# First attention of a six-layer decoder kernel: slot scores made in turned layout, two heads in the two 64-column halves of the array

## The chip, the cores and the metric

One core of a Trainium2 chip. The metric is the device time of one execution of the whole kernel in microseconds (us), as the median over runs.

## The reference, cut to what matters

The kernel computes a decoder with two layers on an input of 4 x 256 tokens of width 256: a gated slot attention, a state-space scan over a context, a mixture of experts, a linear attention, a cross attention and a quantized feed-forward block, each followed by a layer norm. The change is in the first of these, the slot attention with 16 heads, key width 64, value width 128 and 64 slots:

```python
z = cumlogsumexp(s, axis=time)          # s: slot logits, clipped
p, g = exp(s - z), exp(z_prev - z)
hk = hk * g + k_t p_t                   # first recurrence, read by q
ok_t = q_t * scale @ hk                 # one row of 64 slots per head
pv = softmax(ok, axis=slots)
hv = hv * g + p_t v_t                   # second recurrence
ov_t = pv_t @ hv
```

Written without the recurrence: with e = exp(s) and z = the running sum of e over time, ok of a query at time t is (sum over keys up to t of (q.k) e) divided by z, slot by slot. The softmax over slots follows, its weights are divided by z again, and ov is (sum over keys up to t of (w.e) v). So there are two divisions by the same z: one of ok before the maximum, one of the softmax weights before they are used.

## The kernel before, in words

The first attention runs over 8 pairs of heads, `step` once per pair (a loop of 7 and a last one), and each engine has its own `step` with its instructions in a fixed order; semaphores tie them. Woven into the same eight steps, on VectorE, ScalarE and GpSimd, is the scan of the second layer (`scan`, `decay_of`, `drive_of`, `read_of`), four scans of 128 x 1024 in each step. PSUM is used as four areas of two banks: PJ, AB, X and Y.

TensorE, in a step of pair i: it turns eT, the exponentials of the slot logits with the slots of two heads in the partitions, into tokens in the partitions (line 606, into X); ScalarE copies them to `e_tok`. Then it projects values and gates of the eight token tiles, `project_vg(t)` (line 617), into the two banks of PJ in turn, each of which must have been emptied by ScalarE (`v`, `th`) and by VectorE (`gate(t-2)`). After tiles 0 and 1 come eight turns of the logarithm of z (line 629, into Y), then the slot scores (lines 639 to 641, into X): for each sequence and head three products with 128 columns of masked scores `aT` as the stationary operand and 64 columns of `e_tok` streaming, an output with tokens in the partitions. Every float32 product is two instructions here, so these are 48. Then tiles 2 to 7 of `project_vg`, then, once VectorE's `w_ready` has come, eight turns of the weights `okn` (line 651, into Y), which ScalarE copies to `wT`. Then for each sequence `read` (line 582, the second use of scores, eT against wT), VectorE's mask (line 1563) and `mix` (lines 671 to 673), the next pair's `project_qks` (572), turns of the output (692), the output projection (703) and the next pair's scores (582).

ScalarE makes `z_inv` = exp(-ln z) from the turned logarithm (line 1265, 2 x 512 columns), the values and tanh of the gates for each tile, `slot_exp` (line 1271) between tiles 3 and 4, and `wT` (line 1279). The page shows nearly all ScalarE work under line 1216, its helper. The logarithm itself is taken in `log_sums`, at the end of the step before.

VectorE: `gate(0)`, `gate(1)`, the scan of line 1552, then okn = slot scores x z_inv (1588), the maximum over each 64 slots (1590), the subtraction of it (1593), the weights okn = slot_exp x z_inv (1598), the sum (1600) and a small product `eps_sq` (1604), with gates between, then the masks.

GpSimd does the products and sums of the layer-2 scan; in `steps` it waits for `w_ready`, the end of line 1598, before the first `read_of`.

Of the kernel before, what the change touches and what calls it, by code (L numbers as in the profile page):

```python
# [16 lines left out]
P = 128  # L17
# [50 lines left out]
def at(i, per, c):  # L68

    return i * per + c  # L70


def build(nc, a, out):

    with ExitStack() as ctx:
# [3 lines left out]
        def sb(name, shape, dt=F32):  # L79
            return mem[-1].enter_context(nc.sbuf_tensor(name, shape, dt))  # L80
# [33 lines left out]
        zT = sb("zT", [P, TOK])  # L114
        z_inv = sb("z_inv", [P, TILES, P])
        aT = sb("aT", [P, 8, 384])
# [185 lines left out]
        e_copied = sem("e_copied")  # L302
        z_turned = sem("z_turned")
        zi_ready = sem("zi_ready")
        slots_ready = sem("slots_ready")
        slots_shifted = sem("slots_shifted")
        slots_exp = sem("slots_exp")
        w_ready = sem("w_ready")
        tanh_ready = sem("tanh_ready")
# [246 lines left out]
        def _(pe):  # L556
# [40 lines left out]
            def step(i, last_pair):  # L597
# [25 lines left out]

                pe.wait_ge(lnz_ready, at(i, 1, 1))
                pe.wait_ge(scores_masked, at(i, 4, 4))
                for n in range(2):
                    for t in range(4):
                        c = (4 * n + t) * P
                        last = nc.tensor.transpose(ps[:, Y + n, t * P:(t + 1) * P], zT[:, c:c + P], ident[:])
                    last.then_inc(z_turned, 1)  # L630

                pe.wait_ge(e_copied, at(i, 2, 2))
                for b in range(B):
                    for h in range(2):
                        n = 2 * b + h
                        m = slice(M * h, M * h + M)
                        o0 = ps[:, X + b // 2, (b % 2) * 256 + M * h:(b % 2) * 256 + M * h + M]
                        o1 = ps[:, X + b // 2, (b % 2) * 256 + P + M * h:(b % 2) * 256 + P + M * h + M]
                        mm(o0, aT[:, n, 0:P], e_tok[:, 2 * b, m], start=True, stop=True)
                        mm(o1, aT[:, n, P:256], e_tok[:, 2 * b, m], start=True, stop=False)  # L640
                        last = mm(o1, aT[:, n, 256:384], e_tok[:, 2 * b + 1, m], start=False, stop=True)
                last.then_inc(slots_ready, 1)
                for t in range(2, TILES):
                    project_vg(t)

                pe.wait_ge(w_ready, at(i, 1, 1))
                pe.wait_ge(zi_ready, at(i, 2, 2))
                for n in range(2):
                    for t in range(4):
                        r = 4 * n + t  # L650
                        last = nc.tensor.transpose(ps[:, Y + n, t * P:(t + 1) * P],
                                                   okn[:, 2 * r:2 * r + 2, :].rearrange("p a b -> p (a b)"), ident[:])
                    last.then_inc(w_turned, 1)
# [456 lines left out]
        def _(pool):  # L1110
# [14 lines left out]
            def steps(i, last_pair):  # L1125
                def read_of(n):

                    j, e = n // 2, n % 2
                    pool.wait_ge(scanned, at(i, 4, n + 3))
                    G.tensor_tensor(state[:, n % 2], state[:, n % 2], c_row[:, j], ALU.mult).then_inc(read_out, 1)  # L1130
                    pool.wait_ge(read_out, at(i, 4, n + 1))
                    pool.wait_ge(y_added, at(i, 4, n + 1))
                    G.tensor_tensor(y[:, e], y[:, e], state[:, n % 2], ALU.add).then_inc(y_added, 1)  # L1133

                pool.wait_ge(w_ready, at(i, 1, 1))
                read_of(0)
                drive_of(i, 2)
                read_of(1)
                drive_of(i, 3)
                if not last_pair:  # L1140
                    pool.wait_ge(zT_ready, at(i, 1, 2))
                read_of(2)
                if not last_pair:
                    drive_of(i + 1, 0)
                read_of(3)
                if not last_pair:
                    drive_of(i + 1, 1)
# [66 lines left out]
        def _(act):  # L1214
# [15 lines left out]
            def log_sums(i):  # L1230
                act.wait_ge(zT_ready, at(i, 1, 1))
                f(zT[:], zT[:], ACT.Ln).then_inc(lnz_ready, 1)

            def rms(i):
# [16 lines left out]
            def step(i, last_pair):  # L1251
# [10 lines left out]
                for t in range(2):  # L1262
                    values_and_gate(t)
                for n in range(2):
                    act.wait_ge(z_turned, at(i, 2, n + 1))
                    f(z_inv[:, 4 * n:4 * n + 4, :].rearrange("p a b -> p (a b)"), bank(Y + n), ACT.Exp,
                      scale=-1.0).then_inc(zi_ready, 1)
                for t in range(2, 4):
# [6 lines left out]
                for t in range(6, TILES):  # L1275
                    values_and_gate(t)
                for n in range(2):
                    act.wait_ge(w_turned, at(i, 2, n + 1))
                    f(wT[:, n * 512:(n + 1) * 512], bank(Y + n), ACT.Copy).then_inc(wT_copied, 1)
                decay_of(i, 2)  # L1280
# [231 lines left out]
        def _(dve):  # L1512
# [4 lines left out]
            dve.wait_ge(const_set, 3)  # L1517
            CHAIN = 4

# [52 lines left out]
            def step(i, last_pair):  # L1572
                def gate(t):
# [10 lines left out]
                dve.wait_ge(slots_ready, at(i, 1, 1))  # L1584
                dve.wait_ge(zi_ready, at(i, 2, 2))
                okf = okn[:].rearrange("p a b -> p (a b)")
                zif = z_inv[:].rearrange("p a b -> p (a b)")
                V.tensor_tensor(okf, pair(X), zif, ALU.mult).then_inc(vec_step, 1)
                dve.wait_ge(vec_step, at(i, CHAIN, 1))
                V.tensor_reduce(okmax[:], okn[:], AX.X, ALU.max).then_inc(vec_step, 1)  # L1590
                gate(2)
                dve.wait_ge(vec_step, at(i, CHAIN, 2))
                V.tensor_tensor(okn[:], okn[:], okmax[:].unsqueeze(2).to_broadcast([P, TILES * 2, M]),
                                ALU.subtract).then_inc(slots_shifted, 1)

                gate(3)
                dve.wait_ge(slots_exp, at(i, 1, 1))
                V.tensor_tensor(okf, slot_exp[:].rearrange("p a b -> p (a b)"), zif, ALU.mult).then_inc(w_ready, 1)
                gate(4)
                V.tensor_reduce(slot_sum[:], slot_exp[:], AX.X, ALU.add).then_inc(vec_step, 1)  # L1600
                gate(5)
                dve.wait_ge(vec_step, at(i, CHAIN, 3))

                V.scalar_tensor_tensor(out=eps_sq[:], in0=slot_sum[:], scalar=LN_EPS, in1=slot_sum[:], op0=ALU.mult,
                                       op1=ALU.mult).then_inc(vec_step, 1)
                for t in range(6, TILES):
                    gate(t)
                for b in range(B):
                    dve.wait_ge(read_ready, at(i, 4, b + 1))
                    mask(b, PJ if b % 2 else AB).then_inc(read_masked, 1)  # L1610
# [4 lines left out]
                dve.wait_ge(squares_read, at(i, 5, 4))  # L1615
                dve.wait_ge(vec_step, at(i, CHAIN, 4))
                V.scalar_tensor_tensor(out=ss[:], in0=ss[:], scalar=1.0 / DV, in1=eps_sq[:], op0=ALU.mult,  # L1617
# [561 lines left out]
```

## Time and profile before

| | |
|---|---|
| median of 3 runs | 1246.0 us (1245.07 to 1246.68) |
| profiled execution, its time | 1248.33 us |
| profiled execution, its span | 1246.3 us |
| TensorE matmul busy | 971.9 us (78% of the span) |
| VectorE busy | 817.0 us (66%) |
| ScalarE busy | 493.8 us (40%) |
| GpSimd busy | 388.3 us (31%) |
| mean granted TensorE clock | 0.879 of full speed |
| time of the 8 steps of the first attention | about 42 to 502 us of the span |

A row of a timeline is one engine's run of equal instructions: start, length, engine, line, operation, the tiles written and read, the number of instructions, and in brackets how long the engine stood idle before them and what ended that. TensorE's instructions overlap: the next one starts some 0.1 to 0.2 us before the last one ends.

### The profile page before, as it was taken

To read this page: it belongs to the slowest core of one execution; us is meant where nothing else is said; L and a number is where in the kernel's file an instruction comes from. 1 tells how busy PE (TensorE), PEld (TensorE's weight loads), DVE (VectorE), ACT (ScalarE), POOL (GpSimd) and SP (SyncE) were. 2 spreads that over 40 slices of the span, in tenths; PEclk is the share of its full clock that TensorE was granted. 3 is DMA by queue.
4 is the path that set the end of the run, shared out by engine and by line. 5 is a ranking of instruction groups with operands and counts; after the bars stand their busy time and mean duration, and the time that the engine had idled before them with its cause. 6 is when DMAs were issued, how large, how long until landed. Compare 5 with 4: busy or idle time off the path is not lost.

```text
span 1246.3 us, 18394 instructions
## 1 busy us (share of the span) xinstructions
PE 971.9 (78%) x5543; PEld 635.2 (51%) x5543; DVE 817.0 (66%) x1466; ACT 493.8 (40%) x847; POOL 388.3 (31%) x325
## 2 busy tenths in 40 slices
PE   6699999999999997448988788820594785888565
PEld 2466675666666575336655555400374443444433
DVE  5558787786868777875544333257577897465766
ACT  3534445445344444302323223303223443867164
POOL 0126554637456555402433333176101000000000
PEclk9689999999999998669999999955696766989677
DMA  4912111111112110220877887632201000000001
GB/s 150 313 47 75 62 57 52 53 63 59 55 50 85 53 42 1 85 76 17 246 254 238 245 255 234 195 105 81 66 1 67 1 0 1 1 0 1 0 1 34
DMA packets 54931, 106.64 MB, mean 86 GB/s; under 512 B 7433, under 2 KB 27537, under 8 KB 54385
## 3 DMA queue, kind: packets, MB, share of 16 engines
q1 hardware_dynamic: 49329, 90.99, 22.6%
q0 software_dynamic: 5568, 15.21, 4.2%
q8 instruction: 19, 0.31, 0.1%
q14 instruction: 15, 0.12, 0.0%
HBM read 86.61 MB, written 19.56 MB: 85 GB/s over the span
## 4 chain that ended last, share of the span: by engine, by line
PE 41%; DVE 25%; SPq 13%; issue 10%; ACT 5%; POOL 3%; DMA 2%; another core or an unknown queue 0%; DVEq 0%; ACTq 0%; POOLq 0%
PE ps L617 8%; SPq L519 6%; PE ps L703 3%; PE ps L582 3%; PE ps L572 3%; DVE row_max L2010 3%; PE ps L964 3%; SPq L516 2%; SPq L525 2%; SPq L522 2%; DVE state L1552 2%; DVE ss L1617 1%; ACT probT L1216 1%; DVE on L1624 1%; PE ps L1007 1%
## 5 line engine op out<-in xcount | busy, mean ns | idle before, releaser
L1130 POOL TENSOR_TENSOR state<-state,c_row 128x1024 f32<-128x1024 f32 x32 | 77.5, 2420 | 207.3 <-DVE zT L1541 82.6
L617 PE MATMUL ps<-w_vg,xT 128*128 128x512 f32 x256 | 117.8, 613 | 0.0
L802 PE MATMUL ps<-w_gv,xgT 128*128 128x352 f32 x272 | 93.6, 478 | 28.1 <-DMA w_gv<-in_w_gv 27.7
L1123 POOL TENSOR_TENSOR drive<-du,b_row 128x1024 f32<-128x1024 f32 x32 | 89.4, 2795 | 56.0 <-DVE y L1701 56.0
L1563 DVE TENSOR_TENSOR aT<-ps,tri 128x768 f32<-128x768 f32 x64 | 59.2, 954 | 47.1 <-PE ps L582 47.1
L572 PE MATMUL ps<-xT,w_qks 128*128 128x512 f32 x192 | 85.0, 593 | 0.4 <-DMA w_qks<-in_wqks 0.4
L1552 DVE TENSOR_TENSOR_SCAN state<-decay,drive 128x1024 f32<-128x1024 f32 x32 | 83.5, 2611 | 0.0
L1171 POOL DMA_INDIRECT xg<-x_dram,tok_cur x68 | 66.7, 981 | 53.6 <-POOL tok_cur L1168 20.6
L802 PEld LDWEIGHTS ps<-w_gv,xgT 128*128 128x128 f32 x272 | 48.0, 192 | 60.1 <-issue 37.9
L2010 DVE TENSOR_REDUCE row_max<-ps 128x1024 f32 x64 | 73.9, 1218 | 6.9 <-PE ps L979 6.4
L1808 DVE SCALAR_TENSOR_TENSOR g_th<-g_th,ps 128x176 f32<-128x176 f32 x76 | 25.7, 338 | 80.1 <-ACT g_th L1216 66.6
L617 PEld LDWEIGHTS ps<-w_vg,xT 128*128 128x128 f32 x256 | 48.2, 196 | 57.9 <-issue 44.0
L1133 POOL TENSOR_TENSOR y<-y,state 128x1024 f32<-128x1024 f32 x32 | 75.4, 2355 | 2.5
L1216 ACT ACTIVATE g_th<-ps 128x176 f32<-128x176 f32 x76 | 24.1, 318 | 128.0 <-PE ps L802 117.6
L814 PE MATMUL ps<-w_dn,hidT 88*128 88x256 f32 x272 | 71.7, 386 | 3.9 <-DMA w_dn<-in_w_dn 3.9
L1205 POOL COPY v_cols<-x_v 128x64 f32 x32 | 8.6, 271 | 198.7 <-PE ps L1007 180.7
L1216 ACT ACTIVATE probT<-ps 128x1024 f32<-128x1024 f32 x64 | 61.6, 1025 | 13.0 <-PE ps L993 13.0
L753 PE MATMUL ps<-ident,xres 128*128 128x128 f32 x64 | 14.6, 422 | 66.5 <-DVE xres L1717 66.5
L1187 POOL DMA_INDIRECT yg<-y_dram,slot_idx x48 | 49.8, 1038 | 43.3 <-DMA y_dram<-y_out 25.3
L703 PE MATMUL ps<-w_o,oT 128*128 128x256 f32 x256 | 61.8, 391 | 0.0
L1848 DVE TENSOR_SCALAR y_out<-ps 128x256 f32<-128x256 f32 x68 | 28.9, 425 | 48.9 <-PE ps L814 33.0
L1576 DVE SCALAR_TENSOR_TENSOR th<-th,ps 128x256 f32<-128x256 f32 x64 | 26.8, 418 | 50.6 <-ACT th L1216 48.7
(290 smaller groups left out, 2233.0 us busy)
## 6 DMA issues: line engine op xcount, KB each, us to landing
w_gv<-in_w_gv SPq DMA_DIRECT2D x68, 352.0 KB
w_dn<-in_w_dn SPq DMA_DIRECT2D x68, 176.0 KB
y_dram<-y_out SPq DMA_DIRECT2D x68, 128.0 KB
b_row<-x_dbl_dram SPq DMA_DIRECT2D x16, 512.0 KB, 3.6
c_row<-x_dbl_dram SPq DMA_DIRECT2D x16, 512.0 KB, 4.8
y_dram<-blank SPq DMA_DIRECT2D x2, 3584.0 KB, 22.2
w_vg<-in_wvg SPq DMA_DIRECT2D x8, 512.0 KB, 3.3
w_qks<-in_wqks SPq DMA_DIRECT2D x8, 384.0 KB, 3.1
```

The source lines that it names most:

```text
L519: return sp.value_load(expert_row[0:1, bass.ds(i * NJ + j, 1)], min_val=0, max_val=E - 1)
L572: last = mm(bank(PJ + n % 2), w_qks[:, k, part * P:(part + 1) * P], xT[:, k, half * 512:(half + 1) * 512], start=(k == 0), stop=(k == KD - 1))
L617: last = mm(bank(PJ + t % 2), xT[:, k, t * P:(t + 1) * P], w_vg[:, k, :], start=(k == 0), stop=(k == KD - 1))
L703: last = mm(ps[:, X + b % 2, 256 * t:256 * t + 256], oT[:, h, c:c + P], w_o[:, h, :], start=(h == 0), stop=(h == 1))
L802: last = mm(ps[:, 2 * j + 1, 0:2 * F], x_of(k), w[:, k, :], start=(k == 0), stop=(k == KD - 1))
L814: last = mm(ps[:, 2 * j + 1, 256:512], hidT[:, j, f * P:(f + 1) * P], w[:, f, :], start=(f == 0), stop=(f == 1))
L1123: G.tensor_tensor(drive[:, n % 2], du[:, e], b_row[:, j], ALU.mult).then_inc(drive_ready, 1)
L1130: G.tensor_tensor(state[:, n % 2], state[:, n % 2], c_row[:, j], ALU.mult).then_inc(read_out, 1)
L1133: G.tensor_tensor(y[:, e], y[:, e], state[:, n % 2], ALU.add).then_inc(y_added, 1)
L1216: return nc.scalar.activation(out, in_, func, **kw)
L1552: V.tensor_tensor_scan(state[:, n % 2], decay[:, n % 2], drive[:, n % 2], 0.0, ALU.mult, ALU.add).then_inc(scanned, 1)
L2010: V.tensor_reduce(row_max[:, bass.ds(i * 16 + 4 * b, 4)], pair(4 + 2 * (b % 2)).rearrange("p (a k) -> p a k", a=4), AX.X, ALU.max).then_in ...
```

## The change

The slot scores are computed with the operands exchanged: `e_tok` of one head (64 columns) is the stationary operand and the masked scores `aT` stream, 256 columns for the first key tile and 128 for the second. The output is turned (slots in the partitions, tokens along the columns): head 0 in partitions 0 to 63, head 1 in partitions 64 to 127 of the same bank. It goes to Y. There are 16 products instead of 24, and they are issued head by head in turn. z lies in that layout already, so the eight turns of its logarithm and `z_inv` go away: ScalarE inverts zT in place right after the logarithm. VectorE multiplies the scores by it from PSUM (`okT`), TensorE turns okT into X after tile 3 of the projections (eight turns), VectorE takes the maximum and subtracts it straight from PSUM. TensorE turns `slot_exp` itself, not its product with 1/z, and VectorE multiplies by 1/z as it copies the turned weights out of PSUM (two of 512 columns, `wT`), which ScalarE did before. `w_ready` is gone, and with it GpSimd's wait for it.

```diff
                 project_vg(1)
-                pe.wait_ge(lnz_ready, at(i, 1, 1))
                 pe.wait_ge(scores_masked, at(i, 4, 4))
+                pe.wait_ge(e_copied, at(i, 2, 2))
+                for b in range(B):
+                    for t, lo, hi in ((0, 0, 256), (1, 256, 384)):
+                        for h in range(2):
+                            m = slice(M * h, M * h + M)
+                            last = mm(ps[m, Y + b // 2, (b % 2) * 256 + t * P:(b % 2) * 256 + 256],
+                                      e_tok[:, 2 * b + t, m], aT[:, 2 * b + h, lo:hi], start=(t == 0), stop=(t == 1))
+                last.then_inc(slots_ready, 1)
+                project_vg(2)
+                project_vg(3)
+
+                pe.wait_ge(okT_ready, at(i, 1, 1))
                 for n in range(2):
                     for t in range(4):
                         c = (4 * n + t) * P
-                        last = nc.tensor.transpose(ps[:, Y + n, t * P:(t + 1) * P], zT[:, c:c + P], ident[:])
-                    last.then_inc(z_turned, 1)
-                pe.wait_ge(e_copied, at(i, 2, 2))
-                for b in range(B):
-                    for h in range(2):
-                        n = 2 * b + h
-                        m = slice(M * h, M * h + M)
-                        o0 = ps[:, X + b // 2, (b % 2) * 256 + M * h:(b % 2) * 256 + M * h + M]
-                        o1 = ps[:, X + b // 2, (b % 2) * 256 + P + M * h:(b % 2) * 256 + P + M * h + M]
-                        mm(o0, aT[:, n, 0:P], e_tok[:, 2 * b, m], start=True, stop=True)
-                        mm(o1, aT[:, n, P:256], e_tok[:, 2 * b, m], start=True, stop=False)
-                        last = mm(o1, aT[:, n, 256:384], e_tok[:, 2 * b + 1, m], start=False, stop=True)
-                last.then_inc(slots_ready, 1)
-                for t in range(2, TILES):
+                        last = nc.tensor.transpose(ps[:, X + n, t * P:(t + 1) * P], okT[:, c:c + P], ident[:])
+                last.then_inc(ok_turned, 1)
+                for t in range(4, TILES):
                     project_vg(t)
-                pe.wait_ge(w_ready, at(i, 1, 1))
-                pe.wait_ge(zi_ready, at(i, 2, 2))
+                pe.wait_ge(slots_exp, at(i, 1, 1))
...
-                                                   okn[:, 2 * r:2 * r + 2, :].rearrange("p a b -> p (a b)"), ident[:])
+                                                   slot_exp[:, 2 * r:2 * r + 2, :].rearrange("p a b -> p (a b)"), ident[:])
...
-                pool.wait_ge(w_ready, at(i, 1, 1))
...
                 f(zT[:], zT[:], ACT.Ln).then_inc(lnz_ready, 1)
+                act.wait_ge(lnz_ready, at(i, 1, 1))
+                f(zT[:], zT[:], ACT.Exp, scale=-1.0).then_inc(zi_ready, 1)
...
-                for n in range(2):
-                    act.wait_ge(z_turned, at(i, 2, n + 1))
-                    f(z_inv[:, 4 * n:4 * n + 4, :].rearrange("p a b -> p (a b)"), bank(Y + n), ACT.Exp,
-                      scale=-1.0).then_inc(zi_ready, 1)
...
-                for n in range(2):
-                    act.wait_ge(w_turned, at(i, 2, n + 1))
-                    f(wT[:, n * 512:(n + 1) * 512], bank(Y + n), ACT.Copy).then_inc(wT_copied, 1)
...
                 dve.wait_ge(slots_ready, at(i, 1, 1))
-                dve.wait_ge(zi_ready, at(i, 2, 2))
-                okf = okn[:].rearrange("p a b -> p (a b)")
-                zif = z_inv[:].rearrange("p a b -> p (a b)")
-                V.tensor_tensor(okf, pair(X), zif, ALU.mult).then_inc(vec_step, 1)
+                dve.wait_ge(zi_ready, at(i, 1, 1))
+                V.tensor_tensor(okT[:], pair(Y), zT[:], ALU.mult).then_inc(okT_ready, 1)
+                gate(2)
+                gate(3)
+                dve.wait_ge(ok_turned, at(i, 1, 1))
+                turned = pair(X).rearrange("p (a m) -> p a m", m=M)
+                V.tensor_reduce(okmax[:], turned, AX.X, ALU.max).then_inc(vec_step, 1)
                 dve.wait_ge(vec_step, at(i, CHAIN, 1))
-                V.tensor_reduce(okmax[:], okn[:], AX.X, ALU.max).then_inc(vec_step, 1)
-                gate(2)
-                dve.wait_ge(vec_step, at(i, CHAIN, 2))
-                V.tensor_tensor(okn[:], okn[:], okmax[:].unsqueeze(2).to_broadcast([P, TILES * 2, M]),
+                V.tensor_tensor(okn[:], turned, okmax[:].unsqueeze(2).to_broadcast([P, TILES * 2, M]),
                                 ALU.subtract).then_inc(slots_shifted, 1)
-                gate(3)
+                gate(4)
                 dve.wait_ge(slots_exp, at(i, 1, 1))
-                V.tensor_tensor(okf, slot_exp[:].rearrange("p a b -> p (a b)"), zif, ALU.mult).then_inc(w_ready, 1)
-                gate(4)
                 V.tensor_reduce(slot_sum[:], slot_exp[:], AX.X, ALU.add).then_inc(vec_step, 1)
                 gate(5)
...
                 for t in range(6, TILES):
                     gate(t)
+                for n in range(2):
+                    c = slice(n * 512, (n + 1) * 512)
+                    dve.wait_ge(w_turned, at(i, 2, n + 1))
+                    V.tensor_tensor(wT[:, c], bank(Y + n), zT[:, c], ALU.mult).then_inc(wT_copied, 1)
```

## Rows read from the trace of the kernel before

**Rows 1.** Busy time of each engine in one stage of 56 us

```profile
core 0: us, PE busy (x) PEld busy (x) DVE busy (x) ACT busy (x) POOL busy (x), PEclk, DMA share, GB/s
...
206.00:262.00 56.00, 54.37 (x290) 36.84 (x289) 42.65 (x59) 25.92 (x47) 30.22 (x13) 1.00 0.17 59
```

**Rows 2.** Timeline of TensorE in the same stage: start, length, engine, line

```profile
229.10 3.60 PE L617 MATMUL ps<-w_vg,xT 128*128 128x512 f32 x8
232.54 1.04 PE L629 MATMUL ps<-ident,zT 128*128 128x128 f32 x8
233.41 0.33 PE L639 MATMUL ps<-e_tok,aT 128*128 128x64 f32 x2
...
238.72 10.68 PE L617 MATMUL ps<-w_vg,xT 128*128 128x512 f32 x24
249.23 1.04 PE L651 MATMUL ps<-ident,okn 128*128 128x128 f32 x8
250.63 1.58 PE L582 MATMUL ps<-wT,eT 64*128 64x256 f32 x16 [0.36 <-ACT wT L1216]
```

**Rows 3.** Timeline of VectorE in the same stage

```profile
234.01 3.79 DVE L1552 TENSOR_TENSOR_SCAN state<-decay,drive 128x1024 f32<-128x1024 f32 x1
239.02 1.23 DVE L1588 TENSOR_TENSOR okn<-ps,z_inv 128x1024 f32<-128x1024 f32 x1 [1.21 <-PE ps L641]
...
241.74 1.22 DVE L1593 TENSOR_TENSOR okn<-okn,okmax 128x1024 f32<-128x1024 f32 x1
...
245.23 0.41 DVE L1576 SCALAR_TENSOR_TENSOR th<-th,ps 128x256 f32<-128x256 f32 x1
...
247.01 0.86 DVE L1604 SCALAR_TENSOR_TENSOR eps_sq<-slot_sum 128x16 f32<-128x16 f32 x1
```

**Rows 4.** Timeline of ScalarE in the same stage

```profile
223.65 1.06 ACT L1216 ACTIVATE zT<-zT 128x1024 f32<-128x1024 f32 x1 [2.07 <-DVE zT L1541]
...
240.97 0.38 ACT L1216 ACTIVATE th<-ps 128x256 f32<-128x256 f32 x1
...
242.99 1.06 ACT L1216 ACTIVATE slot_exp<-okn 128x1024 f32<-128x1024 f32 x1
...
249.98 1.09 ACT L1216 ACTIVATE wT<-ps 128x512 f32<-128x512 f32 x2
```

**Rows 5.** Timeline of GpSimd in the same stage, and one row of the last step

```profile
235.61 4.34 POOL L1123 TENSOR_TENSOR drive<-du,b_row 128x1024 f32<-128x1024 f32 x1
245.48 2.36 POOL L1130 TENSOR_TENSOR state<-state,c_row 128x1024 f32<-128x1024 f32 x1 [5.53 <-DVE okn L1598]
...
449.73 2.36 POOL L1133 TENSOR_TENSOR y<-y,state 128x1024 f32<-128x1024 f32 x1
```

**Rows 6.** Page, costliest groups: a maximum that VectorE takes from PSUM

```profile
L2010 DVE TENSOR_REDUCE row_max<-ps 128x1024 f32 x64 | 73.9, 1218 | 6.9 <-PE ps L979 6.4
```

**Rows 7.** Timeline of VectorE before the last step: operations that read PSUM

```profile
443.49 0.69 DVE L1635 TENSOR_TENSOR xres<-xres,ps 128x512 f32<-128x512 f32 x1
...
450.94 1.82 DVE L1563 TENSOR_TENSOR aT<-ps,tri 128x768 f32<-128x768 f32 x2 [0.16 <-PE ps L582]
```

**Rows 8.** Timeline of TensorE in the cross attention: products in four 32-column parts

```profile
1059.76 1.07 PE L1007 MATMUL ps<-probT,v_cols 128*32 128x256 f32 x16
...
1060.77 0.90 PE L993 MATMUL ps<-qsT,ksT 64*128 64x256 bf16 x8
```

**Rows 9.** Timeline of TensorE in the first step

```profile
58.30 0.69 PE L639 MATMUL ps<-e_tok,aT 128*128 128x64 f32 x2 [8.65 <-ACT e_tok L1216]
...
68.60 13.16 PE L617 MATMUL ps<-w_vg,xT 128*128 128x512 f32 x24
...
83.00 1.58 PE L582 MATMUL ps<-wT,eT 64*128 64x256 f32 x16 [0.36 <-ACT wT L1216]
```

**Rows 10.** Timeline of VectorE in the first step

```profile
62.17 2.28 DVE L1552 TENSOR_TENSOR_SCAN state<-decay,drive 128x1024 f32<-128x1024 f32 x1
```

**Rows 11.** Busy time and granted clock in two stretches of the first step, columns as above

```profile
66.00:69.00 3.00, 3.00 (x15) 3.00 (x15) 0.06 (x1) 0.00 (x0) 0.00 (x0) 0.50 0.00 0
...
73.00:74.00 1.00, 1.00 (x3) 0.50 (x2) 0.95 (x2) 0.02 (x1) 0.00 (x0) 0.66 0.00 0
```

More of the change, by code:

```diff
@@ L114, in build @@
         zT = sb("zT", [P, TOK])
-        z_inv = sb("z_inv", [P, TILES, P])
+        okT = sb("okT", [P, TOK])
         aT = sb("aT", [P, 8, 384])
@@ L302, in build @@
         e_copied = sem("e_copied")
-        z_turned = sem("z_turned")
+        okT_ready = sem("okT_ready")
+        ok_turned = sem("ok_turned")
         zi_ready = sem("zi_ready")
@@ L307, in build @@
         slots_exp = sem("slots_exp")
-        w_ready = sem("w_ready")
         tanh_ready = sem("tanh_ready")
@@ L1517, in _ @@
             dve.wait_ge(const_set, 3)
-            CHAIN = 4
+            CHAIN = 3
             dve.sem_inc(scanned, 2)
@@ L1584, in step @@
                 dve.wait_ge(slots_ready, at(i, 1, 1))
-                dve.wait_ge(zi_ready, at(i, 2, 2))
-                okf = okn[:].rearrange("p a b -> p (a b)")
-                zif = z_inv[:].rearrange("p a b -> p (a b)")
-                V.tensor_tensor(okf, pair(X), zif, ALU.mult).then_inc(vec_step, 1)
+                dve.wait_ge(zi_ready, at(i, 1, 1))
[5 more added lines that the diff above has]
+                V.tensor_reduce(okmax[:], turned, AX.X, ALU.max).then_inc(vec_step, 1)
                 dve.wait_ge(vec_step, at(i, CHAIN, 1))
-                V.tensor_reduce(okmax[:], okn[:], AX.X, ALU.max).then_inc(vec_step, 1)
-                gate(2)
-                dve.wait_ge(vec_step, at(i, CHAIN, 2))
-                V.tensor_tensor(okn[:], okn[:], okmax[:].unsqueeze(2).to_broadcast([P, TILES * 2, M]),
+                V.tensor_tensor(okn[:], turned, okmax[:].unsqueeze(2).to_broadcast([P, TILES * 2, M]),
                                 ALU.subtract).then_inc(slots_shifted, 1)
-                gate(3)
+                gate(4)
                 dve.wait_ge(slots_exp, at(i, 1, 1))
-                V.tensor_tensor(okf, slot_exp[:].rearrange("p a b -> p (a b)"), zif, ALU.mult).then_inc(w_ready, 1)
-                gate(4)
                 V.tensor_reduce(slot_sum[:], slot_exp[:], AX.X, ALU.add).then_inc(vec_step, 1)
                 gate(5)
-                dve.wait_ge(vec_step, at(i, CHAIN, 3))
+                dve.wait_ge(vec_step, at(i, CHAIN, 2))
                 V.scalar_tensor_tensor(out=eps_sq[:], in0=slot_sum[:], scalar=LN_EPS, in1=slot_sum[:], op0=ALU.mult,
@@ L1615, in step @@
                 dve.wait_ge(squares_read, at(i, 5, 4))
-                dve.wait_ge(vec_step, at(i, CHAIN, 4))
+                dve.wait_ge(vec_step, at(i, CHAIN, 3))
                 V.scalar_tensor_tensor(out=ss[:], in0=ss[:], scalar=1.0 / DV, in1=eps_sq[:], op0=ALU.mult,
```

## The prediction

> **What bounds the kernel now.** I read the busy time by stage first, then the timelines of the four engines over one step. In a stage of 56 us the matmul side is busy 54.37 us at a granted clock of 1.00, VectorE 42.65 us [rows 1]; the reader should see that a step is TensorE work end to end. TensorE's timeline says the same: projections of tiles 0 and 1 from 229.10, the turns of ln z at 232.54, the slot scores from 233.41 to 238.72, six tiles of projection, the turns of the weights at 249.23, and the first real gap, 0.36 us, before `read` at 250.63 [rows 2]. So I look at one stretch only, from 229.10 to the start of `read(0)`, 21.53 us. What follows it (masks, scan, squares, output, next pair) is started by `read(0)` and is not edited, so it shifts as a whole; what precedes it is not edited either, except one ScalarE instruction. The change of a step is the shift of `read(0)`.
>
> VectorE has only 1.21 us of idle time between the end of its scan and the arrival of the slot scores [rows 3]. That is the number to watch: the change makes TensorE deliver earlier, and VectorE can't take it much earlier. The scan is late for its own reason: it starts at 234.01 and takes 3.79 us where the same scan takes 2.28 us when GpSimd is idle [rows 3, 10]; GpSimd's own product beside it takes 4.34 instead of 2.36 [rows 5]. The two take turns, and nothing in the change alters that.
>
> **The change, part by part** (times of the step at 206 to 262).
>
> 1. Turns of ln z removed: 233.41 - 232.54 = 0.87 us of TensorE [rows 2]. They come back as turns of okT, at the same price.
> 2. Slot scores. Before: 48 instructions in 238.72 - 233.41 = 5.31 us, 0.11 us each [rows 2]. After: 32 instructions. A 512-column one takes (249.23 - 238.72) / 24 = 0.438 us [rows 2], so 256 columns take 0.219 and 128 take 0.109; half of the 32 are of each kind, 5.2 us one after another. If the two 64-column halves run side by side it is 2.6. The nearest rows: 16 instructions of 64 rows and 256 or 128 columns in two row halves take 1.58 us with their drain [rows 2], and in the cross attention 16 of 256 columns in four 32-column parts pass in 60.77 - 59.76 = 1.01 us, where one after another would be 3.5 [rows 8]. Column parts do overlap here, by 3.5 of 4. Low bound 2.6, high bound 5.2; I take 2.7, by the row with column parts. TensorE reaches tile 2 at 232.54 + 2.7 = 235.25, tile 3 is through at 238.7.
> 3. okT on VectorE, 1.23 us as line 1588 (one PSUM source, the same size). It can't start before the scan ends at 234.01 + 3.79 = 237.8, so it ends at 239.0, and TensorE waits 0.3 us for it. Turns of okT 239.0 to 239.95, their last result at 240.06 (1.04 us as line 629 [rows 2]).
> 4. Maximum and subtraction from PSUM. Before they read SBUF. Bounds: 1.22 us each as before, and 1.218 us for a maximum over as many elements from PSUM [rows 3, 6]; I take 1.22. Subtraction done at 242.6. Gates 2 and 3 lie in the wait for the turns and cost nothing (two of 0.41 us in 1.1 us); without that cover they'd add 0.8.
> 5. slot_exp: before, the subtraction ended at 242.96 and ScalarE began at 242.99 [rows 3, 4]. Now 242.65, ending at 243.7. ScalarE stands in order in front of tile 4's values, so tile 4 (ready at 241.9) waits: values and tanh take 0.28 + 0.38 us [rows 4], tanh ends at 244.4, gate(4) (0.41 us [rows 3]) at 244.85. Here is **the new wait**: tile 6 needs gate(4), and TensorE, done with tile 5 at 239.95 + 2 x 1.72 = 243.4, stands for 1.5 us. Behind it are tiles 6 and 7 and the turns of the weights, and all of `read`. Tile 7 then needs gate(5), which follows the slot sum (1.2 us) and is done at 246.3, before tile 6 ends. Tiles 6 and 7: 244.88 to 248.3.
> 6. Weights' turns 248.3; slot_exp is long there. wT moves to VectorE: before, `read(0)` began 250.63 - 249.23 = 1.40 us after the turns. Now the last tile's values and tanh end 0.2 + 0.28 + 0.38 = 0.86 after it, gate(7) takes 0.41, then 0.66 for half of wT (line 1635, 0.69, reads PSUM and SBUF at that size [rows 7]; line 1588 halved gives 0.62): 1.93 us. `read(0)` at 250.25. The second half is needed by `read(2)` only; masks start a microsecond later, so it costs nothing.
> 7. Line 1598 (1.2 us) leaves VectorE, in time in which it now waits for exp anyway: nothing. z_inv leaves ScalarE, the inversion of zT comes in: 1.06 us as the logarithm before it at 223.65; ScalarE's next work is 4 us later [rows 4], so nothing; uncovered it would be 1.06.
> 8. GpSimd no longer waits for w_ready: its `read_of(0)` starts at 239.95 instead of 245.48 and it is busy to 247.1 [rows 5]. Nothing on the path waits for it sooner. Its price is what VectorE it holds up: the 16-element eps_sq, 0.86 us before because of it [rows 3], is held to 247.1, and gate(6) isn't due before 247.4: nothing.
> 9. Queues: no DMA is added or moved. SP's load of w_vg follows tile 7, about a microsecond earlier.
>
> Sum for a step: 250.63 - 250.25 = 0.38 us gained. Of TensorE's 2.6 us saved in item 2, it gives back 0.3 for okT, 1.5 for gate(4) and 0.5 for wT. Seven steps: 2.7 us.
>
> **The first step** is another case. There the granted clock is 0.50, that is 1.2 GHz, while the slot scores run, 68.60 - 58.30 = 10.3 us, and it returns to 1.00 only in the stretch 73 to 74, about 5 us into the projections [rows 9, 11]. The new slot scores take 5.2 us at that clock, and the scan is done at 64.45 [rows 10], so projections start at 63.5. If the clock rises as far into them as before, tile 3 is through at 69.4 (tile 2 takes 3.4, tile 3 2.5), the rest is as above: turns 1.0, maximum and subtraction 2.5, exp, tanh and gate(4) 2.2, two tiles 3.4, wT 1.9: `read(0)` at 80.6 instead of 83.00, 2.4 us gained. If it rises at 73.7 as before, the gain is 0.5; if it rises during the denser slot scores, TensorE is ahead and okT bounds: 5. I take 2.4.
>
> Total: 2.7 + 2.4 = 5.1 us. Against the profiled execution, 1248.3 (span 1246.3 and 2.0 around it), that is 1243.2; that execution lies 2.3 above the median of the runs shown, so for the median I forecast 1246.0 - 5.1 = 1241. About 0.2%, 2.5 us, is what a measurement of this kernel can tell from no change.
>
> **Rivals.**
>
> A. *Loads set the pace; no change.* In the slot scores of before an instruction starts every 0.11 us although its 64 columns need half of that: the weight loads set the pace [rows 2]. If a load costs that also in the halves, 32 x 0.11 = 3.6 us. Tile 3 is then through at 239.55, 0.5 later than okT, and `read(0)` at 250.8: 0.14 us lost per step, 1.0 in seven, 0.7 gained in the first. 1246. The break-even for a step is a slot stage of 3.1 us or so, so hand-offs a few tenths longer than mine give the same end. Against it: the 32-column row, 0.063 us per instruction. The Trainium skill, "TensorEngine Tiling (Array Packing)", Restrictions and Gotchas, says that column tiling excludes the fast weight load; it speaks for this case, and with loads at 3.6 us the sum would be no change instead of 5.1 gained. Chance 0.22.
>
> B. *The halves run one after another; slower.* Place: the slot stage. Price: 5.2 us instead of 2.7. Tile 3 is through at 241.2, the turns follow without a wait, subtraction done at 244.8, `read(0)` at 252.3: 1.7 us lost per step, because the chain maximum, exp, gate(4), tile 6 hangs on it. Seven steps 12, the first some 2: 1260. It decides from 3.1 us of slot stage upward, one us per us. For it: the two products write one bank, and each streams through all 128 rows. Against: [rows 8], which do both. Chance 0.12.
>
> C. *GpSimd holds up the chain.* It is now active during maximum and subtraction; if each waited for one of its products, 2 x 2.36 - 0.4 = 4.3 us per step, 1276. Against: two masks reading PSUM from 450.94 take 1.82 together, no more than elsewhere, beside a GpSimd sum running from 449.73 to 452.09 [rows 5, 7]. Chance 0.04, and 0.02 for another loss of a few us.
>
> D. *More gained.* The clock returns early in the first step and hand-offs are shorter: 1236. Chance 0.08.
>
> **How the numbers follow.** The forecast has 0.52. With D that is 0.60 for faster; A is 0.22 for the same; B and C, 0.18, slower. The range runs from D's 1235 over A to 1251, which takes in a first step without gain and half a us lost per step; it leaves out B and C, 0.16 to 0.18.
>
> **What the profile should show.** Slot instructions of form 128*64, 32 per step, started within 2.7 us; okT starting at the scan's end and not at the slots' end; TensorE idle 0.3 us before the turns of okT, 1.5 us before tile 6 with VectorE's gate named, and about 0.9 us before `read(0)` with wT on VectorE; maximum and subtraction at 1.22 us; GpSimd active right after 239.95; a step of 55.5 instead of 55.9 us. A slot stage over 3.1 us, a maximum well over 1.22, or a granted clock under 1.00 in steps 2 to 8 would make the forecast wrong.

## The result and the profile after

The changed kernel takes 1235.98 us in the median (1234.43 to 1237.57, 4 runs) where the kernel before, in the same rounds, took 1245.53. The ratio on record is 0.9936, with a 95% interval of 0.9919 to 0.9953; the two medians alone give 0.9923. It is faster, as forecast, inside the range, and by more than the 5.1 us of the sum. Two later measurements gave 0.9928 (0.9907 to 0.9949) and 0.9942 (0.9929 to 0.9956).

TensorE's timeline of the changed kernel, one step, from the turns (transposes on TensorE) of eT to `read`; it answers to [rows 2]:

```profile
222.94 1.09 PE L606 MATMUL ps<-ident,eT 128*128 128x128 f32 x8
223.87 3.60 PE L617 MATMUL ps<-w_vg,xT 128*128 128x512 f32 x8
227.40 2.82 PE L630 MATMUL ps<-aT,e_tok 128*64 128x256 f32 x32
230.15 3.70 PE L617 MATMUL ps<-w_vg,xT 128*128 128x512 f32 x8
233.74 1.09 PE L640 MATMUL ps<-ident,okT 128*128 128x128 f32 x8
234.67 3.60 PE L617 MATMUL ps<-w_vg,xT 128*128 128x512 f32 x8
239.53 3.70 PE L617 MATMUL ps<-w_vg,xT 128*128 128x512 f32 x8 [1.26 <-DVE th L1568]
243.07 1.04 PE L649 MATMUL ps<-ident,slot_exp 128*128 128x128 f32 x8
245.04 1.58 PE L582 MATMUL ps<-wT,eT 64*128 64x256 f32 x16 [0.94 <-DVE wT L1600]
```

Line 630 is the new slot stage: 32 instructions of form 128*64 in 230.15 - 227.40 = 2.75 us, where 48 took 5.31. Then the two waits that TensorE did not have before: 1.26 us before tile 6, on VectorE's gate, and 0.94 before `read`, on wT. From the turns of eT to `read` it is 245.04 - 222.94 = 22.10 us, against 250.63 - 228.17 = 22.46 before, where the turns of eT are this row:

```profile
228.17 1.09 PE L606 MATMUL ps<-ident,eT 128*128 128x128 f32 x8
```

The turns of eT follow each other every 55.52 us instead of 55.88.

VectorE in the same stretch; it answers to [rows 3]:

```profile
228.78 3.80 DVE L1544 TENSOR_TENSOR_SCAN state<-decay,drive 128x1024 f32<-128x1024 f32 x1
232.49 1.19 DVE L1578 TENSOR_TENSOR okT<-ps,zT 128x1024 f32<-128x1024 f32 x1
...
234.92 1.22 DVE L1583 TENSOR_REDUCE okmax<-ps 128x16 f32<-128x1024 f32 x1
236.17 1.23 DVE L1585 TENSOR_TENSOR okn<-ps,okmax 128x1024 f32<-128x1024 f32 x1
239.06 0.42 DVE L1568 SCALAR_TENSOR_TENSOR th<-th,ps 128x256 f32<-128x256 f32 x1 [1.67 <-ACT th L1213]
...
240.86 0.97 DVE L1593 SCALAR_TENSOR_TENSOR eps_sq<-slot_sum 128x16 f32<-128x16 f32 x1
...
244.30 1.28 DVE L1600 TENSOR_TENSOR wT<-ps,zT 128x512 f32<-128x512 f32 x2
```

There is no idle time between the scan and okT: VectorE takes the slot scores as soon as it can, 2.3 us after TensorE had them (227.40 + 2.82 = 230.22 against 232.49). Maximum and subtraction from PSUM cost what they cost from SBUF: the subtraction of before took 1.22 us, and so did its maximum, here in the last step:

```profile
463.69 1.22 DVE L1590 TENSOR_REDUCE okmax<-okn 128x16 f32<-128x1024 f32 x1
```

ScalarE between them, which answers to [rows 4]:

```profile
234.16 0.38 ACT L1213 ACTIVATE th<-ps 128x256 f32<-128x256 f32 x1
237.42 1.06 ACT L1213 ACTIVATE slot_exp<-okn 128x1024 f32<-128x1024 f32 x1 [2.88 <-DVE okn L1585]
238.39 0.36 ACT L1213 ACTIVATE v<-ps 128x256 f32<-128x256 f32 x1
238.65 0.38 ACT L1213 ACTIVATE th<-ps 128x256 f32<-128x256 f32 x1
```

ScalarE stands idle for 2.88 us in front of slot_exp while tile 4, projected from 234.67 to 236.4, lies ready behind it: the new wait of item 5, as an order of instructions.

The first step, TensorE, answers to [rows 9]:

```profile
58.37 5.30 PE L630 MATMUL ps<-aT,e_tok 128*64 128x256 f32 x32 [9.60 <-ACT e_tok L1213]
63.61 3.70 PE L617 MATMUL ps<-w_vg,xT 128*128 128x512 f32 x8
...
78.50 1.58 PE L582 MATMUL ps<-wT,eT 64*128 64x256 f32 x16 [0.93 <-DVE wT L1600]
```

`read` starts at 78.50 instead of 83.00. The projections after the slot stage run at full clock at once: tiles 2 and 3 take 67.14 - 63.61 = 3.53 us up to the turns of okT, as in later steps. The busy time by stretch names the moment (last three columns: granted clock, DMA share, GB/s); it answers to [rows 11]:

```profile
62.00:63.00 1.00, 1.00 (x10) 0.77 (x8) 1.00 (x2) 0.00 (x0) 0.00 (x0) 0.50 1.04 347
63.00:64.00 1.00, 1.00 (x7) 0.56 (x4) 1.00 (x1) 0.00 (x0) 0.00 (x0) 0.77 1.05 350
```

### The profile page after: what moved, and what is told of

It reads as the page before. It is cut to its first block, busy times and chain, and to the rows that moved or that the text cites. A ratio compares the mean times of both kernels' runs of the same rounds, so it can differ in the third digit from the quotient of the medians.

```text
span 1232.5 us, 18141 instructions
## 1 busy us (share of the span) xinstructions
PE 949.3 (77%) x5415; PEld 599.4 (49%) x5415; DVE 816.3 (66%) x1474; ACT 485.0 (39%) x823; POOL 385.9 (31%) x325
## 4 chain that ended last, share of the span: by engine, by line
PE 37%; DVE 27%; SPq 13%; issue 11%; ACT 5%; POOL 4%; DMA 3%; DVEq 0%; ACTq 0%; POOLq 0%
PE ps L617 6%; SPq L519 6%; PE ps L701 3%; PE ps L582 3%; PE ps L572 3%; PE ps L962 3%; DVE row_max L2003 2%; SPq L516 2%; SPq L525 2%; POOL yg L1184 2%; SPq L522 2%; PE ps L630 2%; DVE state L1544 2%; PE ps L1005 1%; PE ps L977 1%
## 5 line engine op out<-in xcount | busy, mean ns | idle before, releaser
L1128 POOL TENSOR_TENSOR state<-state,c_row 128x1024 f32<-128x1024 f32 x32 | 77.4, 2418 | 200.7 <-DVE state L1544 118.1
L1168 POOL DMA_INDIRECT xg<-x_dram,tok_cur x68 | 66.6, 979 | 53.6 <-POOL tok_cur L1165 38.6
L1801 DVE SCALAR_TENSOR_TENSOR g_th<-g_th,ps 128x176 f32<-128x176 f32 x76 | 25.6, 337 | 78.4 <-ACT g_th L1213 78.3
L701 PE MATMUL ps<-w_o,oT 128*128 128x256 f32 x256 | 61.8, 391 | 0.0
```

Of the source, the lines that this page charges most:

```text
L701: last = mm(ps[:, X + b % 2, 256 * t:256 * t + 256], oT[:, h, c:c + P], w_o[:, h, :], start=(h == 0), stop=(h == 1))
```

## The experiments

Each is an edit of the changed kernel unless it says otherwise. The period is the time between the turns of eT of two neighbouring steps, taken over steps 2 to 8 of the profiled execution.

**1. The halves, not side by side.** The products are ordered so that neighbours use the same half.

```diff
-                for b in range(B):
-                    for t, lo, hi in ((0, 0, 256), (1, 256, 384)):
-                        for h in range(2):
+                for h in range(2):
+                    for b in range(B):
+                        for t, lo, hi in ((0, 0, 256), (1, 256, 384)):
```

> The changed kernel with the slot products ordered head 0 first, then head 1, so that neighbours use the same 64-column half. Theory (the halves run side by side, and TensorE and VectorE arrive level at the turns of okT): the slot stage goes from 2.75 us to 5.2 in steps 2 to 8 and the period of a step from 55.5 to 57.6 to 57.9; the first VectorE idle appears before okT. Rival (VectorE's scan alone sets the start of okT): its slack of 2.2 us swallows most, period 55.5 to 55.8. First step: if the clock rises because columns stream without gaps, it is back at 63 to 64 as in the changed kernel and the first step loses about 2.5 us; if it rises only with both halves in use, the slot stage takes over 10 us and the first step loses 5 or more. Time: theory 1236 + 8 x 2.3 = 1254, rival 1238.

1252.55 us, ratio 1.0049 (1.0032 to 1.0066): slower than the kernel before. The period is 57.52 us, 2.00 more than in the changed kernel and 1.64 more than before. TensorE's and VectorE's timelines:

```profile
233.31 4.82 PE L630 MATMUL ps<-aT,e_tok 128*64 128x256 f32 x32
238.06 3.70 PE L617 MATMUL ps<-w_vg,xT 128*128 128x512 f32 x8
241.60 1.04 PE L640 MATMUL ps<-ident,okT 128*128 128x128 f32 x8
```

```profile
234.69 3.78 DVE L1544 TENSOR_TENSOR_SCAN state<-decay,drive 128x1024 f32<-128x1024 f32 x1
238.40 1.19 DVE L1578 TENSOR_TENSOR okT<-ps,zT 128x1024 f32<-128x1024 f32 x1
```

The same 32 instructions take 4.75 us instead of 2.75. okT still starts at the scan's end and is ready at 239.6, yet its turns start at 241.60: they queue behind tiles 2 and 3. So two things arrive at line 640, okT from VectorE and tile 3 on TensorE itself; in the changed kernel they are level (okT ends at 232.49 + 1.19 = 233.68, the turns start at 233.74), and every us of slot stage beyond its 2.75 shows. In this order the change loses. Two parts of the expectation missed: VectorE has no idle time before okT, since even this stage ends at 238.1, ahead of the scan (238.5), and the period is a little under the 57.6 to 57.9 forecast, because the stage takes 4.75 us and not 5.2.

The clock of the first step does not need the halves side by side. The same stretches:

```profile
62.00:63.00 1.00, 1.00 (x8) 0.71 (x8) 0.66 (x2) 0.73 (x3) 0.64 (x1) 0.84 1.04 343
63.00:64.00 1.00, 1.00 (x11) 0.82 (x8) 1.00 (x2) 0.00 (x0) 0.00 (x0) 1.00 1.08 354
```

It is back during the slot stage here too, and `read` of the first step starts at 80.42. What TensorE had run before it rose was, in both orders, the new products. The eight turns that the change takes out of this stretch are not the cause: experiment 2 puts eight turns back and has the clock up between 63 and 64, experiment 3 keeps the old products and has it up between 71 and 72.

**2. More TensorE work ahead of the slot scores.**

```diff
                 pe.wait_ge(e_copied, at(i, 2, 2))
+                pe.wait_ge(zi_ready, at(i, 1, 1))
+                for n in range(2):
+                    for t in range(4):
+                        c = (4 * n + t) * P
+                        nc.tensor.transpose(ps[:, Y + n, t * P:(t + 1) * P], zT[:, c:c + P], ident[:])
```

> The changed kernel with eight more turns (of zT into Y, overwritten by the slot scores) ahead of the slot scores, 0.93 us of TensorE per step. Theory (TensorE and VectorE level at okT): nearly all of it shows, period 55.5 to 56.3, time 1243. Rival (VectorE bound up to read, TensorE has slack): period 55.5, time 1236.

1243.25 us, ratio 0.9970 (0.9957 to 0.9982); the period is 56.39, 0.87 more for turns that take 0.97 us until the slot products start. TensorE has no slack to give at the turns of okT: they start at 237.58 here, 0.86 us after okT is ready (235.53 + 1.19 = 236.72), against 0.06 us in the changed kernel. That VectorE has none either is read from the changed kernel's timeline, where the scan, okT and its turns follow each other without a gap; no run makes VectorE alone earlier or later. The experiment also prices the eight turns of ln z that the change removed.

**3. The second division alone.** The kernel before, with this part of the change and nothing else (`w_ready` now says that zT is inverted).

```diff
-                pe.wait_ge(w_ready, at(i, 1, 1))
+                pe.wait_ge(slots_exp, at(i, 1, 1))
...
-                                                   okn[:, 2 * r:2 * r + 2, :].rearrange("p a b -> p (a b)"), ident[:])
+                                                   slot_exp[:, 2 * r:2 * r + 2, :].rearrange("p a b -> p (a b)"), ident[:])
...
-                pool.wait_ge(w_ready, at(i, 1, 1))
...
+                f(zT[:], zT[:], ACT.Exp, scale=-1.0).then_inc(w_ready, 1)
...
-                    f(wT[:, n * 512:(n + 1) * 512], bank(Y + n), ACT.Copy).then_inc(wT_copied, 1)
...
-                V.tensor_tensor(okf, slot_exp[:].rearrange("p a b -> p (a b)"), zif, ALU.mult).then_inc(w_ready, 1)
...
+                dve.wait_ge(w_ready, at(i, 1, 1))
+                for n in range(2):
+                    c = slice(n * 512, (n + 1) * 512)
+                    dve.wait_ge(w_turned, at(i, 2, n + 1))
+                    V.tensor_tensor(wT[:, c], bank(Y + n), zT[:, c], ALU.mult).then_inc(wT_copied, 1)
```

> The kernel before with the second division alone moved: TensorE turns slot_exp, VectorE multiplies by 1/z as it copies the turned weights out, ScalarE inverts zT in place after z_inv, GpSimd no longer waits. Theory (this part costs, and the slot stage earns): read starts about 0.5 us later after the turns than with ScalarE's copy, period 55.9 to 56.4, time 1245.5 + 4 = 1249.5. Rival (the freed 1.2 us of VectorE and the earlier GpSimd are worth something): period under 55.9, faster than before.

1249.01 us, ratio 1.0021 (1.0012 to 1.0031); period 56.29, 0.41 more than before. TensorE's timeline:

```profile
249.13 1.04 PE L651 MATMUL ps<-ident,slot_exp 128*128 128x128 f32 x8
251.10 1.58 PE L582 MATMUL ps<-wT,eT 64*128 64x256 f32 x16 [0.93 <-DVE wT L1608]
```

`read` comes 1.97 us after the turns instead of 1.40, and the six tiles ahead of the turns take 10.35 us instead of 10.51: 0.57 - 0.16 = 0.41. This half of the change, which takes a 1.2 us instruction off VectorE and two off ScalarE (and adds the inversion of zT there), costs 0.4 us a step: what it takes away lay beside TensorE's projections, what it adds lies between the last of them and `read`. By subtraction the rest of the change, slot scores and first division, earns 0.36 + 0.41 = 0.77; that part was not run alone, since the second division as before needs z with tokens in the partitions.

**4. GpSimd's wait given back.**

```diff
+                pool.wait_ge(slots_exp, at(i, 1, 1))
                 read_of(0)
```

> The changed kernel with a wait for slots_exp given back to GpSimd ahead of its first read_of of a step. Theory (GpSimd's earlier work costs VectorE nothing on the path): period 55.5, time as changed, 1236. Rival (GpSimd beside maximum and subtraction holds the chain up): period shorter by some tenths. Other rival (the earlier GpSimd work is where gain comes from): period longer by up to 0.4.

1238.13 us, ratio 0.9943 (0.9921 to 0.9965), period 55.51 against 55.52: neither gain nor loss. GpSimd stands idle for 3.92 us, from 235.24 to 239.16, and maximum and subtraction, now with GpSimd idle beside them, take what they take in the changed kernel. Of VectorE's instructions only eps_sq changes its length:

```profile
235.43 1.22 DVE L1584 TENSOR_REDUCE okmax<-ps 128x16 f32<-128x1024 f32 x1
236.68 1.23 DVE L1586 TENSOR_TENSOR okn<-ps,okmax 128x1024 f32<-128x1024 f32 x1
...
241.04 0.41 DVE L1569 SCALAR_TENSOR_TENSOR th<-th,ps 128x256 f32<-128x256 f32 x1
241.37 0.19 DVE L1594 SCALAR_TENSOR_TENSOR eps_sq<-slot_sum 128x16 f32<-128x16 f32 x1
242.76 0.42 DVE L1569 SCALAR_TENSOR_TENSOR th<-th,ps 128x256 f32<-128x256 f32 x1 [1.20 <-ACT th L1214]
```

It takes 0.19 us instead of 0.97. Here it starts at 241.37, and GpSimd's product ends at 241.53; in the changed kernel it starts at 240.86, and it ends, at 241.83, with GpSimd's product (241.79). VectorE then waits that much longer for the tanh. The Trainium skill, "GPSIMD Engine Reference", Key points, says that GpSimd contends with VectorE instructions that have two SBUF inputs. The rows agree: eps_sq reads SBUF twice and is held, maximum and subtraction read PSUM and take 1.22 us with GpSimd busy or idle. The subtraction of experiment 3 reads SBUF twice, as in the kernel before, but with GpSimd now active beside it, and takes 1.60 us instead of 1.22:

```profile
241.80 1.60 DVE L1590 TENSOR_TENSOR okn<-okn,okmax 128x1024 f32<-128x1024 f32 x1
```

**5. Tile 4 ahead of slot_exp on ScalarE.**

```diff
-                for t in range(2, 4):
+                for t in range(2, 5):
                     values_and_gate(t)
                 act.wait_ge(slots_shifted, at(i, 1, 1))
                 f(slot_exp[:], okn[:], ACT.Exp, scale=DK ** -0.5).then_inc(slots_exp, 1)
-                for t in range(4, 6):
+                for t in range(5, 6):
```

> The changed kernel with ScalarE taking tile 4's values and gate ahead of slot_exp. Theory (TensorE's 1.26 us of idle before tile 6 is tile 4 held behind exp, and on the path): idle gone but for 0.3 us before tile 7, period 55.5 to 54.2 to 54.5, time 1236 - 9 = 1227. Rival (the exp itself is what ends last): exp a little later, weights' turns wait instead, period 55.5.

1225.52 us, ratio 0.9836 (0.9818 to 0.9853), period 54.40. TensorE's timeline has the four tiles 4 to 7 in one piece:

```profile
231.42 7.43 PE L617 MATMUL ps<-w_vg,xT 128*128 128x512 f32 x16
238.69 1.04 PE L649 MATMUL ps<-ident,slot_exp 128*128 128x128 f32 x8
```

7.43 us where 16 such instructions need 7.03 (experiment 7): of 1.26 us, 0.4 are left. They lie between 236.4 and 237.2, where tile 7 starts, and gate(5), which it needs, ends at 236.8 behind the slot sum.

**6. The first half of wT ahead of gate(7).**

```diff
-                for t in range(6, TILES):
-                    gate(t)
+                gate(6)
                 for n in range(2):
                     c = slice(n * 512, (n + 1) * 512)
+                    if n:
+                        gate(7)
                     dve.wait_ge(w_turned, at(i, 2, n + 1))
```

> The changed kernel with VectorE making the first half of wT ahead of gate(7) instead of behind it. Theory (read(0) waits 0.94 us for wT, of which 0.6 is the last tile's values, tanh and gate): idle before read 0.3 us, period 54.9, time 1231. Rival (read(1) then waits for gate(7) and masks come no earlier): period 55.3 or more.

1230.97 us, ratio 0.9880 (0.9861 to 0.9899), period 54.93: 0.59 gained, and the idle time before `read` is 0.35 us, as little as it was with ScalarE's copy.

**7. Both, and gate(5) ahead of the slot sum** (experiments 5 and 6 in one kernel, and this).

```diff
+                gate(5)
                 dve.wait_ge(slots_exp, at(i, 1, 1))
                 V.tensor_reduce(slot_sum[:], slot_exp[:], AX.X, ALU.add).then_inc(vec_step, 1)
-                gate(5)
```

> Both of the last two, and gate(5) ahead of the slot sum. Theory: the two waits are in series, 1.26 + 0.6 us, period 53.6 to 53.9, time 1236 - 14 = 1222. Rival (behind them VectorE or GpSimd ends last): period 54.5 or more.

1217.22 us, ratio 0.9794 (0.9772 to 0.9817), period 53.41, which is 2.11 less than the changed kernel and 2.47 less than before, and also less than the 53.6 to 53.9 expected. Experiments 5 and 6 gained 1.12 and 0.59; the other 0.40 is, by subtraction, what gate(5) was worth, and as much as experiment 5 left before tile 7. TensorE's timeline:

```profile
220.05 2.82 PE L630 MATMUL ps<-aT,e_tok 128*64 128x256 f32 x32
222.80 3.70 PE L617 MATMUL ps<-w_vg,xT 128*128 128x512 f32 x8
226.37 1.09 PE L640 MATMUL ps<-ident,okT 128*128 128x128 f32 x8
227.30 7.03 PE L617 MATMUL ps<-w_vg,xT 128*128 128x512 f32 x16
234.17 1.04 PE L649 MATMUL ps<-ident,slot_exp 128*128 128x128 f32 x8
235.55 1.58 PE L582 MATMUL ps<-wT,eT 64*128 64x256 f32 x16 [0.35 <-DVE wT L1601]
```

TensorE has no gap left in this stretch but the 0.35 us before `read`. This version is faster than both kernels: what the slot stage had freed on TensorE was there to be had, behind three places in two queues.

**8. Where the rest of the 9 us is.** The changed kernel twice more, timed; the kernel before profiled twice more.

> The changed kernel once more, beside the kernel before in the same rounds. Theory (all of the gain lies in the first attention, 4.5 us in its first step and 0.36 in each of seven others): 7.0 us less, ratio 0.9944. Rival (something after the attention gains too): 9.5 us or more less, ratio 0.9924 or under.

> The changed kernel, a third profile, and timed beside the kernel before. Theory (7 to 8 us from the attention, the rest scatter): ratio 0.9935 to 0.9945; behind the attention 727 to 735 us; clock back between 61 and 65 of the first step, read at 77 to 79, period 55.52. Rival (something behind the attention gains as well): ratio under 0.993 and under 729 behind the attention.

> The kernel before, a second profile. Theory (what differs behind the attention is scatter between executions): from the first turn after the attention to the end of the span it takes 727 to 735 us, as the nine profiles so far, and the period of a step is 55.88. Rival (the kernel before is slower behind the attention too): 733 or more in each of its profiles.

> The same, a third profile: the same expectations. In the first step the granted clock is back at 1.00 between 71 and 74 and read starts at 82 to 83.

The timed ones gave the two ratios at the top; the three intervals share 0.9929 to 0.9949. The first of them lies between its two expectations: 8.9 us less, where 7.0 and 9.5 or more stood against each other. From three profiles of each kernel, in us:

| | before | changed |
|---|---|---|
| period of a step | 55.88, 55.88, 55.87 | 55.52, 55.52, 55.52 |
| start of `read`, first step | 83.0, 81.4, 83.3 | 78.5, 77.4, 79.0 |
| first turn after the attention | 511.6, 510.1, 511.9 | 504.6, 503.5, 505.1 |
| from there to the end of the span | 734.7, 736.7, 737.0 | 727.9, 733.3, 735.2 |

Up to the end of the attention the kernels differ by 511.2 - 504.4 = 6.8 us, 0.9945, and each profile lies within about a us of its kernel's mean. Behind it nothing was edited, and the changed kernel scatters by 7 us between its own executions. The theory for these profiles, scatter alone and 727 to 735 us in either kernel, did not hold for the kernel before: its two new profiles have 736.7 and 737.0, as the rival (733 or more) had it. The rival for the changed kernel's third, under 729, did not hold either: it has 735.2.

All thirteen profiles together say more. With the new products it is 727.4 to 729.4 us behind the attention in seven of nine profiles and 733.3 and 735.2 in two; with the old ones it is 733.2 to 737.0 in all four. The medians agree: in each of the nine measurements with the new products, the median differs from the kernel before's by 1.2 to 4.8 us more, in their favour, than the end of the attention does in the profile; in experiment 3, which has the old ones, by 0.4. So a few us behind the attention go with the new slot products, and no run shows by which path.

A part of it is the expert outputs' gather, rows of the source view (least, median and longest ns, first and last start), of the kernel before and then of the changed one:

```profile
L1187 POOL DMA_INDIRECT yg<-y_dram,slot_idx x48: 945/949/2879, 808.9 to 875.8; - x48
```

```profile
L1184 POOL DMA_INDIRECT yg<-y_dram,slot_idx x48: 942/946/1984, 802.5 to 864.4; - x48
```

66.9 us before, 61.9 changed. Before, the largest single stop in it is 4.00 us of GpSimd waiting for VectorE's `xres`; the changed kernel's first profile has none over 0.31. It is 66.6 and 66.6 us in the other two profiles of before, 61.9 and 67.1 in the other two of changed, 61.8 to 62.3 in the six other kernels with the new products, and 62.1 in experiment 3, which is slower than the kernel before. So it does not go with the change in each case. Whether and how the change shifts its odds stays open. For the changed kernel alone all that lies behind the attention is worth 1.2 to 3.0 us by the medians, and 0 to 2 us by the ratio between 0.9929 and 0.9949.

## Why the prediction was right, and where it was off

- **The bound.** The chain of a step was as read: TensorE up to `read`, everything behind it shifting as a whole. From `read` to the next turns of eT it is 33.42 us before (55.88 - 22.46) and changed (55.52 - 22.10).
- **Items 1 and 2.** 2.7 us were taken for the slot stage, 2.75 measured; the row with column parts was the right neighbour. The turns cost 0.87 by experiment 2.
- **Item 3.** A wait of 0.3 us for okT was forecast; the two are level within 0.1. TensorE's slack is nil, which experiments 1 and 2 show; VectorE's is read from the timeline.
- **Item 4.** 1.22 and 1.23 us from PSUM, as taken.
- **Item 5.** 1.5 us before tile 6, 1.26 measured. That it is an order on ScalarE and not the exp that ends last is shown by experiment 5.
- **Item 6.** `read` 1.93 us after the turns, 1.97 measured; experiment 3 has the same 1.97 in the kernel before.
- **Items 7 and 8.** Nothing gained, nothing lost: in experiment 3 the instruction that left VectorE earned nothing, and experiment 4 shows that GpSimd's earlier start neither gains nor costs anything.
- **A step.** 0.38 us forecast, 0.36 measured, seven times.
- **The first step** is the term that was mis-sized: 2.4 us forecast, 82.6 - 78.3 = 4.3 measured. The forecast let the clock rise as far into the projections as before, and so gave tiles 2 and 3 3.4 + 2.5 = 5.9 us; they took 3.53. The clock rose during the slot stage or within 0.8 us of its end, in all nine profiles with the new products between 61 and 65, and between 70 and 74 in all four with the old ones. That was the other end of the term's bounds (5), in case D, though not with what bounds it there: okT was ready at 65.5, and its turns waited for TensorE until 67.14.
- **Rival A**, loads that set the pace: no. Its 3.6 us were 32 loads at the old spacing of 0.11; the stage takes 2.75. In the slot stage of before TensorE's weight loads fill all of a stretch of 5.20 us; in the new one they are busy 1.90 us of 2.60, and one takes 137 ns instead of 192. The rule of the Trainium skill, "TensorEngine Tiling (Array Packing)", Restrictions and Gotchas, that column tiling excludes the fast weight load was put behind this rival; no run here shows a load that became slower by it.
- The **break-even** in rivals A and B, a slot stage of 3.1 us, is what the runs give, 2.75 + 0.36. The forecast's own terms give 3.4: 2.7, the 0.3 of waiting for okT and the 0.38 gained. The two come apart because the wait of 0.3 did not occur.
- **Rival B** did not occur; experiment 1 brings it about. It took 1.7 us a step for a stage of 5.2 us; measured are 1.64 for one of 4.75. That they agree is luck: beyond the break-even it costs one us per us, as B says, and 5.2 us would have cost 2.1. Its first step was wrong: `read` 2.2 us earlier than before where 2 later was taken, again by the clock. The end of the attention comes 520.5 - 511.2 = 9.3 us later and the median is 6 us longer, not 14.
- **Rival C**: no, by experiment 4.
- **The total.** The sum of 5.1 becomes 6.8 with what its two terms measured, 2.5 for seven steps and 4.3 for the first. The medians differ by 9.5, 8.9 and 7.8 us in the three measurements; the 1.0 to 2.7 us beyond 6.8 lie behind the attention, where the forecast had no term, and are not explained. That 1236 is also case D's figure is in part luck: its early clock occurred, its shorter hand-offs did not, and what filled their place is this unexplained part. The range held the result a us above its lower end.

## What to carry to other kernels

Exchanging the operands and putting two heads in the two column halves of TensorE halved this stage of 64-column products, 5.31 to 2.75 us, with neighbours in the queue in different halves; with the order of the loops the other way it was 4.75. When TensorE gets faster ahead of a softmax, look at what stands in the queues of ScalarE and VectorE behind the maximum and the exp: of 2.6 us freed in a step, 0.36 arrived, and three small reorderings in two queues brought 2.11 more. An operation that left a busy engine earned nothing, because it lay beside the bound, and the one that replaced it, between the last turn and `read`, cost 0.57 us a step.

## What the runs showed that was not expected

In the first step TensorE was never idle from 58.3 until the clock was back, in either kernel. Yet it stayed at 1.2 GHz for the whole old slot stage (10.3 us) and some 2 to 5 us of projections behind it, and with the new products, serial or side by side, it was back at 2.4 GHz by the end of their stage or just behind it. Busy time in the profile was the same, without a gap, in both. Why the one stage brought the clock back and the other did not is open. The gain of about 2 us from it was not to be seen from the busy share.

The serial order takes 4.75 us for 32 instructions; by the 0.219 and 0.109 us an instruction of item 2 it would be 5.2. Where the half microsecond comes from is open.
